# A table of 16-byte rows in place of scattered token rows, and attention's rows added in HBM

## The reference, cut to what matters

```
xn  = layernorm(x)
out = x + attention(xn) + experts(xn)

attention: 16 heads of 16; q = (xn Wq + bq) / 4, k, v; softmax over 1024 keys of q k^T plus a learned
           term for the 9 nearest positions; probs v, plus the same 9 probabilities times emb_rel_v; Wo, bo
experts:   logits = xn gate_w + gate_b; the two best of 8 by softmax, weights made to sum to 1
           h = silu(xn w1[e]) * (xn w3[e]);  out += weight * (h w2[e])      (F = 1024)
```

## Time and profile before

| | us |
|---|---|
| median of 3 runs | 1824.39 (1821.48 to 1829.11) |
| the profiled execution's own time | 1838.71 |
| its span in the trace | 1837.0 |
| TensorE busy | 1694.4 (92%) |
| VectorE busy | 1437.7 (78%) |
| ScalarE busy | 1099.4 (60%) |
| GpSimd busy | 826.2 (45%) |

### The profile page before, as it was taken

How to read it: one execution, slowest core, us unless ns; L and a number is a source line. 1 busy time by engine, 2 the same in 40 slices (tenths; PEclk the granted TensorE clock), 3 DMA queues, 4 the chain that set the end, 5 groups by cost and what they waited for, 6 DMA issues and landing times. The chain is left out here.

```text
span 1837.0 us, 35484 instructions
## 1 busy us (share of the span) xinstructions
PE 1694.4 (92%) x13756; PEld 1022.4 (56%) x13756; DVE 1437.7 (78%) x2540; ACT 1099.4 (60%) x2133; POOL 826.2 (45%) x595
## 2 busy tenths in 40 slices
PE   5998799999999999999998999999999999999991
PEld 3774223333333333333334778888788888788880
DVE  3556979998887788878675998999989999987652
ACT  3664548887877778777586545454455454455540
POOL 3001000049889988899421445544445544442120
PEclk9997759999999999999698999999999999999995
DMA  5999316646666566565134777777777777666745
GB/s 166 349 334 278 62 18 147 164 100 150 169 160 159 154 166 161 139 156 145 36 118 145 225 227 237 239 245 248 222 238 230 250 245 237 220 211 193 210 121 189
DMA packets 195752, 342.69 MB, mean 187 GB/s; under 512 B 33392, under 2 KB 145920, under 8 KB 187392
## 3 DMA queue, kind: packets, MB, share of 16 engines
q1 hardware_dynamic: 159264, 212.61, 41.1%
q0 software_dynamic: 27744, 106.84, 19.2%
q10 hardware_dynamic: 8576, 20.97, 3.2%
HBM read 277.27 MB, written 62.83 MB: 185 GB/s over the span
## 5 line engine op out<-in xcount | busy, mean ns | idle before, releaser
L1193 DVE CUSTOM_DVE_ANT_0 w2s<-t_s,hide 128x1024 bf16<-128x1024 f32 x512 | 607.2, 1221 | 129.6 <-PE t_s L1048 110.0
L1328 ACT ACTIVATE t_pr<-t_s 128x512 f32<-128x512 f32 x1024 | 559.4, 604 | 186.7 <-PE t_s L1062 132.8
L1048 PE MATMUL t_s<-ks,qs 48*128 48x512 f16 x1024 | 373.4, 419 | 41.6 <-DVE t_mx L1193 25.5
L1677 ACT ACTIVATE e_sg<-e_pa,down 128x256 f32<-128x256 f32 x312 | 147.7, 473 | 399.6 <-PE e_pa L1568 395.5
L1058 PE MATMUL t_s<-qs,ks 50*128 50x512 f16 x1024 | 366.0, 402 | 10.4 <-ACT t_pr L1328 7.9
L1075 PE MATMUL t_po<-t_pr,t_vx 128*32 128x256 f32 x4096 | 348.6, 413 | 0.5 <-issue 0.3
L1577 PE MATMUL e_py<-w2s,e_hT 128*128 128x256 f32 x1248 | 323.2, 382 | 0.0
L1748 DVE SCALAR_TENSOR_TENSOR ks<-big,up,qs 128x512 f16<-128x512 f32 x304 | 310.5, 1032 | 13.5
L1506 POOL DMA_INDIRECT expert_sums<-e_y,e_token x78 | 140.5, 1801 | 293.1 <-DMA expert_sums<-e_y,e_token 203.7
L1568 PE MATMUL e_pa<-xh,qs 128*128 128x256 f16 x1248 | 240.3, 274 | 20.7 <-DVE xl L1740 17.9
L1568 PE MATMUL e_pa<-xl,qs 128*128 128x256 f16 x1248 | 239.7, 274 | 0.0
(11 more groups left out here) (243 smaller groups left out, 1980.2 us busy)
## 6 DMA issues: line engine op xcount, KB each, us to landing
big<-in_L_ffn_w_dram SPq DMA_DIRECT2D x78, 1024.0 KB, 5.0
w2s<-in_L_ffn_w_dram SPq DMA_DIRECT2D x39, 1024.0 KB
big<-k_rows POOLq DMA_DIRECT2D x32, 1152.0 KB
e_vs<-v_rows POOLq DMA_DIRECT2D x32, 1152.0 KB, 6.0
big<-in_L_ffn_w_dram ACTq DMA_DIRECT2D x16, 1024.0 KB, 7.5
qs<-q_parts SPq DMA_DIRECT2D x96, 128.0 KB, 4.4
ks<-k_parts SPq DMA_DIRECT2D x96, 128.0 KB, 5.9
slot_rows<-t_zero SPq DMA_DIRECT2D x13, 780.0 KB, 11.8
```

The lines of the kernel that those rows point to most:

```text
L1048: last = nc.tensor.matmul(s1[:, buf, half * CH:(half + 1) * CH], qs[lows, u, h, i * P:(i + 1) * P], ks[lows, u, h, half * CH:(half + 1) * ...
L1193: nc.vector.tensor_tensor_reduce(out=seen[:, buf, :], in0=s1[:, buf, :], in1=c["hide"][:, (TB - 1 - row) * P:(TB - 1 - row) * P + L], scal ...
L1328: nc.scalar.activation(pr[:, k % BP, n % HG], s2[:, turn(u, n)], ACT.Exp, scale=SPREAD ** -2).then_inc(exp_ok, 1)
```

## The change: what it does

`slot_rows` (39 x 256 rows of 1040 bytes) becomes `slot_table` (as many rows of 16 bytes: token number, two weights, expert). It is zeroed, or rather filled with the numbers of spare rows, by two transfers of SyncE with 4992 pieces of 16 bytes each; two spare tiles are also zeroed behind `xn_rows`. GpSimd no longer brings normed rows to SBUF for sending; it scatters 16-byte rows. When all are sent, SyncE loads the whole table to SBUF in two parts (16 and 62 of its 78 tiles of 128 rows), GpSimd makes the token numbers integers and gathers the normed rows of slots 0 and 1 by them, and does `ones` after that. In the expert stage GpSimd gathers each next slot's rows with two indirect transfers; SyncE's load of them is gone; the gates of all slots are made once, in slot 0. The second transfer of `put` no longer waits for the first to land, since the two halves of a slot have spare tiles of their own. Each finished tile of attention is added to `expert_sums` by an indirect transfer, after both of `put` have landed. `combine` is gone: SyncE copies `expert_sums` to the output from HBM to HBM, 8 transfers of 128 pieces of 4096 bytes.

```diff
-        xn=dram("xn_rows", [T, E], F32),
+        xn=dram("xn_rows", [T + ST * P, E], F32),
-        xs=dram("slot_rows", [NS * TS, XE], F32),
-        moe=dram("expert_sums", [T + P, E], F32),
+        slots=dram("slot_table", [NS * TS, 4], F32),
+        moe=dram("expert_sums", [T + ST * P, E], F32),
...
+def gather_rows(nc, dr, xr, token, came, s, u):
+    for i in range(ST):
+        nc.gpsimd.indirect_dma_start(
+            out=xr[:, u, i, 0:E], out_offset=None, in_=dr["xn"],
+            in_offset=bass.IndirectOffsetOnAxis(ap=token[:, s * ST + i:s * ST + i + 1], axis=0)).then_inc(came[u], 16)
...
# attention, SyncE: zeroing
-                for z in range(N_ZERO // 2):
-                    sp.dma_start(zeros[z], zero[:].broadcast_to([P, 6, XE])).then_inc(zero_out, 16)
+                for i in range(ST):
+                    sp.dma_start(zeros[i], zero[:, i:i + 1, E:XE].broadcast_to([P, NS, XE - E])).then_inc(zero_out, 16)
+                sp.dma_start(dr["xn"][T:T + ST * P].rearrange("(i p) e -> p i e", p=P), zero[:, :, 0:E]).then_inc(zero_out, 16)
                 step(1, 0, 3, 1)
-                for z in range(N_ZERO // 2, N_ZERO):
-                    sp.dma_start(zeros[z], zero[:].broadcast_to([P, 6, XE])).then_inc(zero_out, 16)
...
# attention, SyncE: its end
                 load_split(0, 0)
                 load_split(0, 1)
-                for u in range(2):
-                    sp.wait_ge(sent[u], 16 * NT)
-                sp.dma_start(xr[:, 0], slot_rows[0]).then_inc(x_in[0], 16)
+                sp.wait_ge(sent, 32 * NT)
+                slots_v = dr["slots"].rearrange("(n p) f -> p n f", p=P)
+                for i, part in enumerate((slice(0, CHUNK), slice(CHUNK, NS * ST))):
+                    sp.dma_start(tab[:, part], slots_v[:, part]).then_inc(tab_in[i], 16)
                 sp.wait_ge(mx_ok, NG * X1)
                 sp.wait_ge(vx_ok, NG)
                 load_second(0)
-                sp.dma_start(xr[:, 1], slot_rows[1]).then_inc(x_in[1], 16)
                 load_second(1)
...
# attention, GpSimd: send(t), two a tile
                     for k in range(2):
                         nc.gpsimd.indirect_dma_start(
-                            out=dr["xs"], out_offset=bass.IndirectOffsetOnAxis(ap=dst[:, t, k:k + 1], axis=0),
-                            in_=xn[:, m % 2, t % CT, :], in_offset=None).then_inc(sent[m % 2], 16)
+                            out=dr["slots"], out_offset=bass.IndirectOffsetOnAxis(ap=dst[:, t, k:k + 1], axis=0),
+                            in_=meta[:, t, :], in_offset=None).then_inc(sent, 16)
...
# attention, GpSimd: after the last send
-                for u in range(2):
-                    pool.wait_ge(sent[u], 16 * NT)
+                for i, part in enumerate((slice(0, CHUNK), slice(CHUNK, NS * ST))):
+                    pool.wait_ge(tab_in[i], 16)
+                    nc.gpsimd.tensor_copy(token[:, part], tab[:, part, 0]).then_inc(token_ok, 1)
+                    pool.wait_ge(token_ok, i + 1)
+                    if i == 0:
+                        for n in range(2):
+                            gather_rows(nc, dr, xr, token, x_in, n, n)
                 nc.gpsimd.memset(ones[:], 1.0).then_inc(ones_ok, 1)
...
# expert stage, SyncE
                 def load(s, u):
-                    sp.dma_start(xr[:, u], xs[s]).then_inc(x_in[u], 16)
...
                 slots(sp, slot)
+                sp.wait_ge(r_out, 16 * NT)
+                sp.wait_ge(y_out[0], 32 * ((NS + 1) // 2))
+                sp.wait_ge(y_out[1], 32 * (NS // 2))
+                for n in range(NC):
+                    sp.dma_start(out_v[n], sums_v[n]).then_inc(o_out, 16)
+                sp.wait_ge(o_out, 16 * NC)
...
# expert stage, GpSimd
                 def put(s, u, k):
-                    pool.wait_ge(gate_ok, s + 1)
                     pool.wait_ge(y_ok, s + 1)
                     if not isinstance(s, int) or s > 0:
                         pool.wait_ge(y_out[1 - u], 32 * (k + u))
+                    after(pool, r_out, 16 * min(s, NT))
                     for i in range(ST):
-                        if i > 0:
-                            pool.wait_ge(y_out[u], 32 * k + 16 * i)
                         nc.gpsimd.indirect_dma_start(
-                            out=dr["moe"], out_offset=bass.IndirectOffsetOnAxis(ap=token[:, u, i:i + 1], axis=0),
+                            out=dr["moe"], out_offset=bass.IndirectOffsetOnAxis(ap=token[:, s * ST + i:s * ST + i + 1], axis=0),
                             in_=y[:, u, i, :], in_offset=None, compute_op=ALU.add).then_inc(y_out[u], 16)
+
+                def add_rows(t, u, k):
+                    pool.wait_ge(res_ok, t + 1)
+                    pool.wait_ge(y_out[u], 32 * (k + 1))
+                    nc.gpsimd.indirect_dma_start(
+                        out=dr["moe"], out_offset=bass.IndirectOffsetOnAxis(ap=rows_at[:, t:t + 1], axis=0),
+                        in_=res[:, u, :], in_offset=None, compute_op=ALU.add).then_inc(r_out, 16)
...
                 def slot(s, u, k, tiles=True):
+                    if 0 < s < NS - 1:
+                        pool.wait_ge(xt_ps, s)
+                        gather_rows(nc, dr, xr, token, x_in, s + 1, 1 - u)
                     if tiles:
                         pool.wait_ge(e_ok, s + 1)
                         products(s, u, k)
                     if not isinstance(s, int) or s > 0:
                         put(s - 1, 1 - u, k if u else k - 1)
+                        if s <= NT:
+                            add_rows(s - 1, 1 - u, k if u else k - 1)
...
# expert stage, VectorE: rows_of(s, u, k), four small instructions in every slot, becomes gates(), three, in slot 0 alone
                     for f in range(FC):
-                        if f == 2:
-                            rows_of(s, u, k)
+                        if f == 2 and first:
+                            gates()
...
# the last stage, combine(), goes
-        combine(nc, dr, oa[:].rearrange("p n h v -> p n (h v)")[:, :, 0:E], out)
```

122 lines of the change are left out of this document (45 added, 77 removed).

## The result

The changed kernel took 1803.1 us (median of four runs, 1783.8 to 1805.1), the kernel before 1822.9 us beside it; the ratio is 0.9877, 95% interval 0.9828 to 0.9926. I had forecast 1825 us and no change. The profiled execution after took 1802.47 us (span 1800.7) against 1838.71 (span 1837.0). The execution profiled before lies 15.8 us above its kernel's median, so the 36.3 us between the two profiles overstate the 19.9 us between the medians.

The account below looks back on a forecast made before the run. TensorE was taken to set the pace of the expert stage, with attention's engines all close to it; 0 + 12 - 5 - 6.5 = +0.5 us moved the 1824.4 us median to about 1825, range 1802 to 1850 for 8 in 10.

Parts of the forecast that it names:

- Part 1: Zeroing and sending in attention: removed transfers and row loads are hidden because GpSimd was early; value 0, bounds 0 and +6.
- The fill: 9984 pieces of 16 bytes written in attention: 11 to 34 us against 33 us of cover before SyncE's next work; 0 to +6.
- Part 2: End of attention: `ones` stands behind the table's load, so TensorE waits for it; +12 us, bounds +7 to +32.
- Part 3: Expert stage: VectorE without `rows_of` delivers `xl` 0.73 us earlier, ending TensorE's 0.56 us waits; with part 4, -5 us.
- Part 4: Expert stage: GpSimd's gathers and landings make 20.6 us a slot, eating most of part 3; together -5, bounds -18 to +20.
- Part 5: End of the span: SyncE starts 6.5 us earlier, the HBM-to-HBM copy still takes 26.8 us; -6.5, bounds -18 and +5.
- third rival: All the gains come: GpSimd keeps up (-15), the copy takes bytes once (-17), `ones` waits 9; -23, 1801 us; chance 0.28.

Follow-up runs that it names:

- fat_fill: The changed kernel with the table filled by one transfer of 39 pieces of 4 KB instead of two of 9984 pieces of 16 bytes: 1826.6 us.
- wide_rows: The changed kernel with 1040-byte rows scattered again, loads of normed rows between the sends, and the 16-byte fill kept: 612 us for the 13 attention groups.
- put_first: The changed kernel with GpSimd's additions of the outputs issued ahead of the window's loads in each expert slot: expert stage 806.0 us.
- late_burst: The changed kernel with its bursts of six sends left whole but issued one band tile (12.5 us) later: 1871 us.

## Why the prediction was wrong

**Part 1 (0, "a gain is excluded, as no engine waits for the zeroing") is the step that failed.** In the first pair of profiles the 13 groups took 583.4 us instead of 622.0, 38.6 less, where this part had 0 to +6. I asked which engine waits for the removed work and found none, and counted the sends as the same 64 instructions. What I did not ask is what six of them in a row do to engines that don't wait for them. The trace of before had the sign, in two rows of its waits that I read past. The waits in them of 1.5 us or more all stand in or right behind a burst of four or six:

```profile
DVE w2s L1193 <- remote: 15.9, 8, 3.7
ACT t_pr L1328 <- remote: 12.3, 6, 3.0
```

The cleanest measure is the kernel before with its sends in pairs, on one chip: 1817.4 us against 1837.6, 20 us less, and 597.2 us for the 13 groups against the 622.0 of its first profile. In the changed kernel the bursts cost what the run makes of them: its 13 groups took 583.4 us with no stop, 598.4 with three of ten (fat_fill), 631.1 with four and 643.5 with six, against 592.3 with the sends in pairs. These are single profiles, partly from different chips. In the first result the whole of attention came out 21 us shorter than before, with the fill and the wait for `ones` in it; in the repeats 39 and 16 us longer. So the sign of this term is not the change's own, and why the first profile was free of stops stays open. That the pauses for row loads broke up some of the bursts before, and made it steadier, fits wide_rows (612), but no run shows it alone.

**The fill, bounded at 0 to +6.** It took 5 us more than the group of before in the first profile (51.3 against 46.2), 6 and 7 in the two others. The landing itself stayed between my two prices: 43 to 48 ns a piece on an engine, 27 to 30 us in all, against 17 and 54 ns, and inside the 33 us of cover. So running out of cover was not the way in which it cost. It held the DMA engines for half of the group and SyncE's issuing for 27 us, and TensorE stopped on "issue" beside it; which of these lengthens the group was not tried apart. Part of the 5 us is also the lower clock at the head of the group, 7 us of it in the first profile against 5 before.

**Part 2 (+12; bounds +7 to +32).** Mechanism right, size off. Measured: a wait of 7.3 us, and 8 to 9 us with the lower clock behind it. The whole load took 10.8 us from its first piece to its last, 17 ns a piece on an engine instead of my 22, and its second part about 16 ns (7936 pieces, 496 an engine, in 8 us between the two casts of 916.00 and 923.95). For the 0.7 us from there to the semaphore I had no row; it was 0.4. The four gathers did not decide, although the wait equals my lower bound: they were over at 921.3, and GpSimd waited 2.67 us more for the second part.

```profile
920.32 0.95 POOL L141 DMA_INDIRECT rows<-xn_rows,rows  x1 [0.30 <-issue]
923.95 0.28 POOL L1024 CAST rows<-rows 128x62 int32<-128x62 f32 x1 [2.67 <-DMA rows<-slot_table]
924.29 0.19 POOL L1029 MEMSET t_ones<- 16x128 f32 x1
```

The rule of the Trainium skill, DMA: Bandwidth & Descriptors, section Bandwidth (about 10.5 ns a small packet, which I took for one engine's), gave +7 because the gathers would decide. The trace has its number, but not its way; the measured 17 ns lies between its figure and my 22.

**Parts 3 and 4 (-5; bounds -18 to +20).** Measured +2.6. Part 3 read "PE waits for xl, 0.56 us" as lateness that VectorE's removed 0.73 us would cure. Two kernels with and without these steps differ by 0.6 us. Part 4 had GpSimd's round right: its gathers cost 1.07 us in the mean, its landings 6.1 us instead of 5.2, and its round came to 21.0 us with no other wait. But it was hardly the pace. With GpSimd relieved (put_first) the round stayed at 20.98 us and the stage gave back 3 to 6 us, not 18. The 20.5 us a slot at which TensorE was to run alone never came.

**Part 5 (-6.5; bounds -18 and +5).** Mechanism right, size off. The earlier start is as worked out: from the first add of the last slot to the first transfer 12.5 us before, 5.6 after, -6.9. The mis-sized term is the copy: 26.8 us to 16.1, which fits bytes that count once (11.5 us less by my working, 10.7 measured). I had taken reads plus writes at 365 GB/s as the limit. The prediction had itself named a copy much shorter than 27 us as a sign that it is wrong. The Trainium skill, DMA: Bandwidth & Descriptors, section Latency and other measured facts, gives 207 to 214 GB/s for copies between HBM tensors whose rows stand at a large pitch; here 4.19 MB, contiguous on both sides, took 16.1 us from issue to end, 260 GB/s with the latencies in it. For this copy the page's figure was too low, and the measurement decides.

**The sum.** The terms as measured in steady stages, +5 (fill), +8 (`ones`), +3, -18, give -2 against my +0.5. That the two are near is luck: the fill and the experts came out 5 and 8 us dearer than forecast, the wait for `ones` 4 us cheaper and the end 11. The 20 us by which the first result was faster and the 17 us by which the second was slower lie for the most part in the 13 groups with the bursts, and no run splits them further. The first result also lies 2 us from my third rival (1801, "all the gains come"), and that is chance too: of that rival's gains the copy came, GpSimd's part did not, and what made up the sum was in no rival.

## What to carry to other kernels

Count what an instruction does to engines that do not wait for it: an unexplained wait ("remote", "issue") that keeps turning up behind the same GpSimd instructions is a cost, and a lower clock mostly follows it. Issue such scatters in pairs between other GpSimd work, not six in a row. And before believing 1%, run the changed kernel again, on another chip too: here the same program was 1.2% faster once and 0.7% slower the next time, each with an interval that excluded the other.

## What the runs showed of the hardware

- Six scatters of 128 rows in a row on GpSimd (0.97 us each, 0.3 apart): VectorE, ScalarE or both wait for 1.5 to 4.7 us on "remote" near the last sends in 57 of 118 bursts (from none of ten in the first profile to nine of ten in late_burst), and TensorE behind them. Four in a row did it in 8 of 25 cases, two in none of 140. What they wait for is not settled. It is not bandwidth: during the stop in the second profile, from 448 to 452 us, the DMA engines moved 2 GB/s, 96 packets in 4 us.

```profile
DMA packets 96, 0.01 MB, mean 2 GB/s; under 512 B 96, under 2 KB 96, under 8 KB 96
```

- Of the 57 bursts with such a stop, 53 are followed by TensorE at 1.2 GHz, for 3 to 20 us, mostly 3 to 14; both together make a group of 44 to 45 us one of 47 to 53, at worst 59.
- Stores of 16 bytes to HBM side by side took 43 to 48 ns a piece on an engine in the three profiles of the changed kernel; 1040 bytes apart 19 ns (wide_rows); loads of 16-byte pieces side by side 15 to 17 ns.
- A copy from HBM to HBM in pieces of 16 KB (256 packets, 4.19 MB) took 16.1 us from the first issue to the end, the same through SBUF 24.0.
